# Causal attention, two items of a head pair in one slot of TensorE's order

## What is computed

```python
def _L1_attn_ref(x, Wq, Wk, Wv, Wo):        # 16 query heads, 4 key/value heads, head width 64
    q = (x @ Wq).reshape(b, t, HKV, G, HD)  # G = 4 query heads share one key/value head
    k = (x @ Wk).reshape(b, t, HKV, HD)
    v = (x @ Wv).reshape(b, t, HKV, HD)
    scores = jnp.einsum('bqhgd,bkhd->bhgqk', q, k) / jnp.sqrt(jnp.float32(HD))
    scores = jnp.where(causal, scores, NEG)
    attn = jax.nn.softmax(scores, axis=-1)
    ctx = jnp.einsum('bhgqk,bkhd->bqhgd', attn, v).reshape(b, t, HQ * HD)
    return ctx @ Wo
...
x = x + _L1_attn_ref(_layernorm(x, axis=-1), L1_attn_Wq, L1_attn_Wk, L1_attn_Wv, L1_attn_Wo)
```

## Time and profile before

| | |
|---|---|
| times of three executions | 1030.67 (median), 1028.32, 1035.21 us |
| profiled execution, first to last instruction | 1028.4 us |
| TensorE matmul records, share of that span | 925.0 us, 90% |
| VectorE, ScalarE, GpSimd | 761.6, 624.5, 510.8 us |
| first and last score product of the stage (start) | 526.3 and 848.0 us |

### The profile page before, as it was taken

How to read it: one execution, slowest core, us unless ns; L and a number is a source line. 1 busy time by engine, 2 the same in 40 slices (tenths; PEclk the granted TensorE clock), 3 DMA queues, 4 the chain that set the end, 5 groups by cost and what they waited for, 6 DMA issues and landing times. The chain is left out here.

```text
span 1028.4 us, 20270 instructions
## 1 busy us (share of the span) xinstructions
PE 925.0 (90%) x6146; PEld 480.8 (47%) x6146; DVE 761.6 (74%) x1656; ACT 624.5 (61%) x1500; POOL 510.8 (50%) x847
## 2 busy tenths in 40 slices
PE   3999999999999997899889999999999997888296
PEld 1222222222332334565455555555555564567296
DVE  7799899889999976889745666666656665676464
ACT  4388888888888883233266665665566652354164
POOL 6366666776554462100144454455445443775544
PEclk8599999999999999999999999999999997696599
DMA  4099920000000000000060000000000000000240
GB/s 103 1 237 245 245 60 1 2 1 2 2 1 0 0 1 1 1 1 1 8 206 6 15 9 7 8 13 5 8 5 13 0 2 1 0 2 16 89 122 19
DMA packets 50684, 37.49 MB, mean 36 GB/s; under 512 B 15737, under 2 KB 48677, under 8 KB 50608
## 3 DMA queue, kind: packets, MB, share of 16 engines
q1 hardware_dynamic: 48864, 32.83, 13.4%
q0 software_dynamic: 1744, 3.72, 1.1%
HBM read 15.54 MB, written 21.45 MB: 36 GB/s over the span
## 5 line engine op out<-in xcount | busy, mean ns | idle before, releaser
L725 DVE TENSOR_REDUCE a_nmax<-a_rows 128x2 f32<-128x1024 f32 x256 | 299.7, 1218 | 26.5 <-PE a_rows L439 23.6
L979 ACT ACTIVATE a_probs<-a_turned 128x512 f32<-128x512 f32 x512 | 270.0, 605 | 48.2 <-PE a_turned L465 46.9
L1451 POOL TENSOR_TENSOR a_prob<-a_prob,a_rinv 128x256 f32<-128x256 f32 (+3 forms) x128 | 159.4, 1253 | 163.9 <-DVE a_rinv L1647 163.6
L1640 DVE TENSOR_REDUCE a_nmax<-a_score 128x2 f32<-128x256 f32 (+3 forms) x128 | 105.6, 825 | 116.5 <-PE a_score L1497 112.2
L1594 ACT ACTIVATE a_prob<-a_score,a_nmax 128x128 f32<-128x128 f32 (+3 forms) x256 | 132.6, 523 | 81.9 <-DVE a_nmax L1640 81.3
L465 PE MATMUL a_turned<-a_q,a_qk 32*128 32x512 bf16 x512 | 136.9, 389 | 7.3 <-ACT a_probs L979 4.9
L424 PE MATMUL a_acc<-a_probs,a_vg 128*32 128x512 f32 x1024 | 138.1, 611 | 0.2
L439 PE MATMUL a_rows<-a_qk 32*128 32x512 bf16 x512 | 108.9, 398 | 5.9 <-DVE a_nmax L725 3.9
L465 PEld LDWEIGHTS a_turned<-a_q,a_qk 32*128 32x128 bf16 x512 | 34.9, 91 | 153.8 <-ACT a_probs L979 125.8
L1494 PE MATMUL a_score<-a_k_s,a_q_s 64*128 64x384 f32 (+3 forms) x512 | 103.7, 481 | 2.2 <-ACT a_prob L1594 1.3
L1653 DVE COPY a_pt<-a_turn 128x128 f32<-128x128 f32 (+3 forms) x224 | 92.2, 447 | 1.4 <-PE a_turn L1508 1.4
(11 more groups left out here) (351 smaller groups left out, 1580.7 us busy)
## 6 DMA issues: line engine op xcount, KB each, us to landing
xs_sorted<-a_blank SPq DMA_DIRECT2D x9, 1935.0 KB
m_m_w<-L_ffn_w SPq DMA_DIRECT2D x8, 512.0 KB, 9.2
c_xs<-xs_sorted SPq DMA_DIRECT2D x23, 129.0 KB, 2.1
g_a_wq<-L_attn_Wq SPq DMA_DIRECT2D x32, 64.0 KB, 2.1
g_X<-x SPq DMA_DIRECT2D x4, 256.0 KB, 4.7
a_wgu<-L_ffn_gate_up_proj SPq DMA_DIRECT2D x1, 1024.0 KB, 5.5
a_wdn<-L_ffn_down_proj SPq DMA_DIRECT2D x1, 512.0 KB, 6.8
g_a_wk<-L_attn_Wk SPq DMA_DIRECT2D x8, 64.0 KB, 1.9
```

The source lines that it names most:

```text
L725: dve.tensor_reduce(nmax[i % 2][:, p // 2, (p % 2) * 2:(p % 2) * 2 + 2], rows[n % 2][:, :, :], AX_X, ALU.max, negate=True).then_inc(row_ou ...
L979: act.activation(probs[:, (tb % 2) * 4 + j, :], turned[n % 3][:, :], ACT.Exp, scale=float(HD0) ** -0.5).then_inc(turn_out, 1)
L1451: pool.tensor_tensor(pr, pr, spread(rinv[:, t % RING, :], 2, width), ALU.mult).then_inc(scl, 1)
L1640: dve.tensor_reduce(nmax[:, t % RING, :], score[t % 2][:, :, 0:width], AX_X, ALU.max, negate=True).then_inc(mx, 1)
```

## The change

The eight items of a unit become four slots (`STEPS1`) of two items each, A (even) and B (odd). The blocks of a pair come in the order 0, 3, 1, 2, so that a slot has blocks 0 and 3 or blocks 1 and 2. In a slot TensorE does the mask of A, the scores of A, the scores of B, the mask of B: the mask is now the first product of A's sum and the last of B's. Behind that come the transposes of the items three before, both items one directly behind the other. The other products of a unit move to new places in the slots, `pv_of` of the first pair into the next unit. VectorE's order in a slot is: maxima of A, reciprocal of the B before, maxima of B, copies of the first transposed item, reciprocal of A, copies of the second. ScalarE's is: exponentials of A, its copy of the first item, exponentials of B, then the rest. `turn_of`, `pv_of`, `y_of`, `project`, the copies themselves, LAG, the ring and all buffers stay as they are.

```diff
--- before.py
+++ after.py
@@ -1298,7 +1298,8 @@
 UNITS1 = B * HKV
 PAIRS = GROUP // 2
 ITEMS = PAIRS * SB
-BLOCKS = (0, 1, 2, 3)
+BLOCKS = (0, 3, 1, 2)
+STEPS1 = ITEMS // 2
 
 
 def both(i): return i % 4 // 2
@@ -1481,22 +1482,30 @@
             pe.wait_ge(v_ev, NT)
             pe.wait_ge(cz, 2)
 
-            def scores_of(i, r, it):
+            def mask_of(i, r, it, first):
+                t, sb = ITEMS * i + it, BLOCKS[it % SB]
+                if first:
+                    wait(pe, ex, 2 * (t - 1) + 2 * ALL_IT * r)
+                for j in range(2):
+                    last = pe.matmul(score[t % 2][:, j, sb * P:(sb + 1) * P], g.ident16[:, :], causal[:, :],
+                                     start=first, stop=not first, skip_group_check=True)
+                if not first:
+                    last.then_inc(s_s, 1)
+
+            def scores_of(i, r, it, first):
                 t, sb, p = ITEMS * i + it, BLOCKS[it % SB], it // SB
                 width = (sb + 1) * P
-
-                wait(pe, ex, 2 * (t - 1) + 2 * ALL_IT * r)
+                if first:
+                    wait(pe, ex, 2 * (t - 1) + 2 * ALL_IT * r)
                 if it % SB == 0:
 
                     pe.wait_ge(pje, projection(i, 1 + p) + 1 + ALL_PJ * r)
                 for j in range(2):
                     h = slice(HD1 * j, HD1 * j + HD1)
-                    pe.matmul(score[t % 2][:, j, 0:width], q_s[i % 2][p][h, sb * P:(sb + 1) * P],
-                              k_s[i // 2 % 2][h, 0:width], start=True, stop=False)
-                for j in range(2):
-                    last = pe.matmul(score[t % 2][:, j, sb * P:width], g.ident16[:, :], causal[:, :],
-                                     start=False, stop=True)
-                last.then_inc(s_s, 1)
+                    last = pe.matmul(score[t % 2][:, j, 0:width], q_s[i % 2][p][h, sb * P:(sb + 1) * P],
+                                     k_s[i // 2 % 2][h, 0:width], start=first, stop=not first, skip_group_check=True)
+                if not first:
+                    last.then_inc(s_s, 1)
 
             def turn_of(i, r, it):
 
@@ -1534,31 +1543,37 @@
             pe.wait_ge(wo_in, 64)
 
             def body(i, r):
-                for it in range(ITEMS):
+                for p in range(STEPS1):
                     if has_unit(i):
-                        scores_of(i, r, it)
-                    back, it2 = unit_of(i, it - LAG)
-                    if has_unit(back) and back >= 0:
-                        turn_of(back, r, it2)
-                    if it == 1 and has_unit(i):
-
-                        pe.wait_ge(pje, projection(i, 2) + ALL_PJ * r)
-                        project(i, r, 2)
-                    if it == 3 and has_last(i):
-                        pv_of(i - 1, r, 1)
-                    if it == 5 and has_last(i):
-                        if has_unit(i):
-                            pe.wait_ge(pje, projection(i, 2) + 1 + ALL_PJ * r)
-                        y_of(i - 1, r)
-                    if it == 7 - i % 2 and has_next(i) and has_last(i):
-                        pe.wait_ge(ye, i + TURN * r)
-                    if it == 6 and has_next(i) and i % 2:
+                        mask_of(i, r, 2 * p, True)
+                        scores_of(i, r, 2 * p, False)
+                        scores_of(i, r, 2 * p + 1, True)
+                        mask_of(i, r, 2 * p + 1, False)
+                    if p == 1 and has_next(i) and i % 2:
                         pe.wait_ge(pje, projection(i + 1, 0) + ALL_PJ * r)
                         project(i + 1, r, 0)
-                    if it == 7 and has_next(i):
+                    if p == 3 and has_last(i):
+                        if has_next(i):
+                            pe.wait_ge(pje, projection(i + 1, 1) + 1 + ALL_PJ * r)
+                        y_of(i - 1, r)
+                    for it in (2 * p, 2 * p + 1):
+                        back, it2 = unit_of(i, it - LAG)
+                        if has_unit(back) and back >= 0:
+                            turn_of(back, r, it2)
+                    if p == 0 and has_last(i) and i < N:
+                        pv_of(i - 1, r, 0)
+                    if p == 0 and has_unit(i):
+
+                        pe.wait_ge(pje, projection(i, 2) + ALL_PJ * r)
+                        if has_last(i):
+                            wait(pe, ye, i - 1 + TURN * r)
+                        project(i, r, 2)
+                    if p == 1 and has_next(i):
                         pe.wait_ge(pje, projection(i + 1, 1) + ALL_PJ * r)
                         project(i + 1, r, 1)
-                    if it == 7 and has_unit(i):
+                    if p == 2 and has_last(i):
+                        pv_of(i - 1, r, 1)
+                    if p == 3 and i == N - 1:
                         pv_of(i, r, 0)
 
             run(pe, body)
@@ -1608,23 +1623,26 @@
                 act.activation(ct[p][:, :], acc[:, :], ACT.Copy).then_inc(cte, 1)
 
             def body(i, r):
-                for it in range(ITEMS):
-                    back, it2 = unit_of(i, it - LAG)
-                    if has_unit(back) and back >= 0:
-                        for j in range(2):
-                            if by_act(j, BLOCKS[it2 % SB]):
-                                copy_turn(back, r, it2, j)
-                    if has_unit(i):
-                        exp_of(i, r, it)
-                    if it == 1 and has_unit(i):
+                for p in range(STEPS1):
+                    for it in (2 * p, 2 * p + 1):
+                        if has_unit(i):
+                            exp_of(i, r, it)
+                        back, it2 = unit_of(i, it - LAG)
+                        if has_unit(back) and back >= 0:
+                            for j in range(2):
+                                if by_act(j, BLOCKS[it2 % SB]):
+                                    copy_turn(back, r, it2, j)
+                    if p == 0 and has_last(i) and i < N:
+                        copy_context(i - 1, r, 0)
+                    if p == 0 and has_unit(i):
                         copy_projection(i, r, 2)
-                    if it == 3 and has_last(i):
+                    if p == 1 and has_next(i) and i % 2:
+                        copy_projection(i + 1, r, 0)
+                    if p == 1 and has_next(i):
+                        copy_projection(i + 1, r, 1)
+                    if p == 2 and has_last(i):
                         copy_context(i - 1, r, 1)
-                    if it == 6 and has_next(i) and i % 2:
-                        copy_projection(i + 1, r, 0)
-                    if it == 7 and has_next(i):
-                        copy_projection(i + 1, r, 1)
-                    if it == 7 and has_unit(i):
+                    if p == 3 and i == N - 1:
                         copy_context(i, r, 0)
 
             run(act, body)
@@ -1653,19 +1671,27 @@
                 dve.tensor_copy(pt[p][j][:, 0:sb + 1, sb * P:(sb + 1) * P],
                                 turn[j][:, 0:(sb + 1) * P].rearrange("p (a s) -> p a s", s=P)).then_inc(copied[j], 1)
 
+            def copy_turns(i, r, it):
+                back, it2 = unit_of(i, it - LAG)
+                if has_unit(back) and back >= 0:
+                    for j in range(2):
+                        if not by_act(j, BLOCKS[it2 % SB]):
+                            copy_turn(back, r, it2, j)
+
             def body(i, r):
-                for it in range(ITEMS):
+                for p in range(STEPS1):
                     if has_unit(i):
-                        max_of(i, r, it)
-                    back, it2 = unit_of(i, it - 1)
+                        max_of(i, r, 2 * p)
+                    back, it2 = unit_of(i, 2 * p - 1)
                     if has_unit(back) and back >= 0:
                         invert(back, r, it2)
-                    back, it2 = unit_of(i, it - LAG)
-                    if has_unit(back) and back >= 0:
-                        for j in range(2):
-                            if not by_act(j, BLOCKS[it2 % SB]):
-                                copy_turn(back, r, it2, j)
-                    if it == 5 and has_last(i):
+                    if has_unit(i):
+                        max_of(i, r, 2 * p + 1)
+                    copy_turns(i, r, 2 * p)
+                    if has_unit(i):
+                        invert(i, r, 2 * p)
+                    copy_turns(i, r, 2 * p + 1)
+                    if p == 3 and has_last(i):
 
                         b = batch_of(i - 1, r)
                         dve.wait_ge(ys, i + TURN * r)
```

## The result

| | median us | ratio to the kernel before | 95% interval |
|---|---|---|---|
| before | 1030.49 | 1 | |
| changed | 1091.13 | 1.0594 | 1.0556 to 1.0632 |

The account below looks back on a forecast made before the run. TensorE was taken to bound the kernel: 74.7 us of added transpose waits, less 19.8 for saved entries and 2 for the queries' wait, gave 53 us more, 1084 us. The range was 1056 to 1108.

Parts of the forecast that it names:

- TensorE's line sets the time: Whole stage: TensorE sets the pace at 20.67 us a unit, so a change is worth what it does there.
- The waits, 74.7 us: Second item's transposes wait for copies of the first: 4.63 us per even unit, 5.01 per odd, 74.7 in all.
- m: The end of a slot's second mask on TensorE, from which the forecast counts its times.
- The term for the maxima ahead of the copies: Slots 0 and 2: B's maxima precede X's copies on VectorE; loss 1.10 us, or 0.83 were VectorE free at once.
- The saved entries, 19.8 us: Eight 64-row entries a unit become four; 0.31 us per entry and exit, 64 over 16 units, 19.8 us saved.
- just covered: Slot 3: B's exponentials end about m+3.9, needed about m+4.1 by the next unit; if not covered, 0.1 to 0.3 a unit.
- The price of the stage's end: Rival: each of 62 slots waits only 0.56 us, as at the stage's end; 35 less 21.8, 1044 us; chance 0.08.
- Entries that stay: Rival: the array empties at each item's first load even inside the form, nothing saved; 1104 us; chance 0.04.
- The clock: Rival: waits of 1 to 1.5 us a slot drop TensorE's clock to 1.2 GHz; 1111 us; chance 0.08.
- The other side, not slower: Rival: copies run under TensorE's other work, only saved entries show; 1009 us, break-even 0.35 us a slot; chance 0.03.

Follow-up runs that it names:

- masks back: Changed kernel, but each item's mask behind its own scores, so the 64-row form is entered eight times a unit again; 1107.14 us, ratio 1.0733.
- The cut product: Changed kernel with other TensorE products between the two items' transposes, plus each unit's second product by the values made in two visits; 1039.97 us, ratio 1.0044.
- the run with the copies first: Changed kernel, but in slots 0 and 2 VectorE copies the first transposed item before the second item's maxima; 1090.68 us, ratio 1.0535.

## Why the prediction was right, and where it was short

- **TensorE's line sets the time: right.** Every kernel's time followed the periods read from TensorE's rows. One row of the waits before was left out of the reading: the weight loads of scores waited 14 times for the exponentials, 10.6 us in all. No matmul's row names them.
- **The waits, 74.7 us: right, and a little too long.** From m to the next product, slot by slot: 2.45, 2.47 or 3.55, 2.45 (slot 2, 656.65 to 659.10) and 3.61 (slot 3, 883.47 to 887.08; 3.94 from 663.02 to 666.96, where the scores wait too). Like for like, at the end of the transposes' stream, slots 0 and 2 have 2.35 against 2.41, slot 1 2.30 against 2.36; slot 3 has 3.60 against 3.59. By my estimate that is some 2.5 us less over the stage. The cause of the waits was isolated from both sides: pushed together in the old kernel the transposes cost 7.1%, pulled apart in the new one they give back all of the 6%. The term for the maxima ahead of the copies (1.10 against 0.83) measured 0.25 instead of 0.27.
- **The saved entries, 19.8 us: the mis-sized term.** The price was right: 0.31 for an entry with its exit, measured 0.31 in the slots where nothing is shared (0.28 and 0.29 as means of four, in two runs). But I took that price for all eight. In the kernel before two of them stood right behind `pv_of`, which works in a form of its own, 64 columns wide:

```profile
613.94 0.49 PE L1494 MATMUL a_score<-a_k_s,a_q_s 64*128 64x128 f32 x4
614.36 0.28 PE L1497 MATMUL a_score<-a_causal,g_ident 128*128 128x128 bf16 x2
```

From 611.63 to 613.94 is 2.31 us for a record of 2.37, of which 0.17 lies behind the stream: 0.11 empty, once, for `pv_of`'s exit and the entry together. With masks back, an entry in that place was worth 0.21, not 0.31. In the changed kernel `pv_of` still takes 2.30 (645.66 to 647.96, 659.10 to 661.40), followed by a projection or a mask in the full form. In slot 0 the projection's weight load, which before started 0.10 us ahead of its product (607.13 and 607.23), starts with it (647.96) and lies open, with nothing else running: 1.13 where it is 1.02. So, by estimate from these rows, 2 x 0.10 + 0.11 a unit were not saved, 5 us, and 14.9 of the 19.8 are left. The cut product shows the price of a visit to the 64-column form by itself, 0.25 to 0.26. The Trainium skill (TensorEngine Tiling (Array Packing), Key Properties) says that changing the tiling mode drains the engine; these runs agree for both forms, with 0.31 and 0.25 a visit.
- **The rest of the 7.6 us** between 53 and 60.6 (5 from the entries, 2.5 back from the waits) is by estimate: the projection behind the waiting transposes of slot 1 starts 0.17 us behind the end of their stream in even units, and has an open load too (1.12 at 678.38), some 3 us over the stage; and two odd units of seven start with a wait for the exponentials (0.16 at 666.96, and the odd period 25.36 instead of 25.03), 0.7 us, at the place that I had as "just covered". The last 1.4 us are less than the runs can settle. So the forecast came out 7 us from the result partly because errors of either sign met.
- **The rivals.** The price of the stage's end (0.56 a slot) was too low, as argued: the slots have larger copies, and maxima ahead. Entries that stay: no, 0.31 each where nothing is shared. The clock: 1.00 throughout the stage, so waits of this length between other products didn't lower it; it did fall once in the run with the copies first, behind the scores' wait of 1.43 us in the first unit. The other side, not slower, had its break-even at 0.35 us a slot; the measured waits are near 1.1.

## What to carry to other kernels

Count a form's changes along the whole order, not per visit: taking out an entry that shares its emptying with another form's exit saves that much less, here 0.21 us instead of 0.31. And what a merge puts side by side matters more than what it saves: two producers of one single buffer back to back wait for the whole hand-over (0.20 out, the copy, 0.17 back), so give each such pair another product of TensorE's to run between, one that lasts as long as the copies and what stands ahead of them in their engine's order. Here the merge with the transposes side by side lost 6%, and the same merge with the products dealt out gained 0.7%.

## What the hardware showed that I had not expected

A transpose that waits for a semaphore leaves the weight load of what follows it open too: the projection behind the waiting transposes has a record of 1.12 us (678.38, its weight load starting 0.01 ahead of it), behind others 1.02 (its weight load 0.10 ahead). And the stages before this one, which no kernel here touches, ended up to 9 us apart between the profiled executions of these kernels (first score product at 524.6 to 533.7), which is more than most of the edits tried here are worth; only the repeating units made them visible.
